# One group in seven fetches its source rows by matmul instead of by gather

## What is computed

```python
def _L0_gnn_ref(h, weight, w_comp, self_loop_weight, A1_w, A1_b, A2_w, A2_b, rel_emb, src, dst, etype):
    x = h[src]                       # one source row of 32 features per edge
    y = h[dst]
    msg = jnp.einsum('eb,ebo->eo', w_comp[etype], jnp.einsum('ei,bio->ebo', x, weight))
    x_hat = x @ A1_w.T + A1_b
    y_hat = y @ A2_w.T + A2_b + rel_emb[etype]
    a = jnp.tanh(jax.nn.relu(jnp.sum(x_hat * y_hat, axis=-1) / scale))
    nei = jax.ops.segment_sum(a[:, None] * msg, dst, num_segments=N)
    last_e = jax.ops.segment_max(jnp.arange(E, dtype=jnp.int32), dst, num_segments=N)
    curr = h[src[last_e]] @ self_loop_weight
    return jax.nn.relu(jnp.where((in_deg > 0)[:, None], nei + curr, jnp.zeros_like(nei)))
```

## Time and profile before

| | |
|---|---|
| three runs | 1352.35, 1353.69 (median), 1355.46 us |
| the profiled execution, its own time | 1355.84 us |
| its span, first to last instruction | 1354.0 us |
| mean granted TensorE clock in it | 0.635 |
| busy: PE, DVE, ACT, POOL | 943.7, 926.2, 636.1, 756.1 us |
| sweep, first fetch to the flag's last step | 75.5 to 1013.7 us |
| instructions | 53620 |

### The profile page before, as it was taken

How to read it: one execution, slowest core, us unless ns; L and a number is a source line. 1 busy time by engine, 2 the same in 40 slices (tenths; PEclk the granted TensorE clock), 3 DMA queues, 4 the chain that set the end, 5 groups by cost and what they waited for, 6 DMA issues and landing times.

```text
span 1354.0 us, 53620 instructions
## 1 busy us (share of the span) xinstructions
PE 943.7 (70%) x21540; PEld 843.1 (62%) x21540; DVE 926.2 (68%) x3188; ACT 636.1 (47%) x1731; POOL 756.1 (56%) x793
## 2 busy tenths in 40 slices
PE   3268777666666666666666666666664696999997
PEld 3257666555555555555555555555554696899997
DVE  8279988666776667667666666666754798555556
ACT  1147766545555555455455545455559783000000
POOL 5777777777777777777777777777750000000000
PEclk9556756555555555555555555555556898999999
DMA  4622111111111111111111111111100000000000
GB/s 99 80 56 55 41 41 40 46 45 39 38 36 33 39 40 40 40 39 40 39 40 39 39 39 40 39 40 39 18 12 14 2 4 2 4 4 4 5 4 17
DMA packets 58572, 44.98 MB, mean 33 GB/s; under 512 B 41920, under 2 KB 54560, under 8 KB 58320
## 3 DMA queue, kind: packets, MB, share of 16 engines
q1 hardware_dynamic: 33296, 28.65, 7.6%
q0 software_dynamic: 25024, 12.86, 6.4%
HBM read 38.37 MB, written 3.07 MB: 31 GB/s over the span
## 4 chain that ended last, share of the span: by engine, by line
POOL 41%; issue 21%; PE 16%; DVE 13%; DMA 6%; SPq 2%; ACT 1%; DVEq 0%; POOLq 0%; ACTq 0%
POOL arena L541 41%; PE ps L757 12%; DMA arena<-line_table 2%; DMA arena<-x_pad,arena 2%; DVE arena L1199 2%; DVE arena L1364 1%; DVE arena L1384 1%; PE ps L680 1%; DVE arena L1197 1%; PE ps L728 1%; DMA agg_table<-arena 1%; SPq L442 1%; DMA dst_parts<-arena 1%; DVE arena L1227 1%; PE ps L626 1%
## 5 line engine op out<-in xcount | busy, mean ns | idle before, releaser
L541 POOL DMA_INDIRECT arena<-x_pad,arena x782 | 754.3, 965 | 238.6 <-issue 236.2
L661 PE MATMUL ps<-arena 128*128 128x175 bf16 (+3 forms) x1567 | 199.1, 297 | 199.6 <-DVE arena L1199 199.1
L680 PE MATMUL ps<-arena 128*32 128x44 f32 (+3 forms) x7832 | 239.8, 262 | 96.2 <-DVE arena L1227 96.1
L661 PEld LDWEIGHTS ps<-arena 128*128 128x128 bf16 x1567 | 146.7, 131 | 217.5 <-DVE arena L1199 216.3
L680 PEld LDWEIGHTS ps<-arena 128*32 128x32 f32 x7832 | 182.1, 156 | 142.9 <-DVE arena L1227 122.5
L1199 DVE TENSOR_SCALAR arena<-pair_no,arena 128x275 bf16<-128x275 f16 (+2 forms) x784 | 237.3, 307 | 0.0
L952 ACT ACTIVATE arena<-arena 128x4 f32<-128x4 f32 x196 | 40.3, 206 | 384.7 <-DVE arena L1213 382.1
L1212 DVE TENSOR_TENSOR arena<-ps,arena 128x132 f32<-128x132 f32 x196 | 57.5, 294 | 238.2 <-DMA arena<-x_pad,arena 235.1
L757 PE MATMUL ps<-arena,adj_words 128*128 128x64 f16 (+1 forms) x6250 | 195.3, 193 | 24.2 <-DVEq L1314 20.9
L757 PEld LDWEIGHTS ps<-arena,adj_words 128*128 128x128 fp8e4 x6250 | 193.1, 98 | 26.2 <-DVEq L1314 21.6
L1227 DVE TENSOR_TENSOR arena<-ps,arena 128x768 f32<-128x768 f32 x196 | 187.9, 959 | 6.7
(11 more groups left out here) (196 smaller groups left out, 1095.0 us busy)
## 6 DMA issues: line engine op xcount, KB each, us to landing
arena<-line_table SPq DMA_DIRECT2D x28, 602.0 KB
arena<-x_pad,arena POOLq DMA_INDIRECT x782, 3.3
arena<-line_table SPq DMA_DIRECT2D x28, 140.0 KB
arena<-dst_parts SPq DMA_DIRECT2D x196, 5.7 KB
agg_table<-arena SPq DMA_DIRECT2D x196, 2.5 KB
dst_parts<-arena SPq DMA_DIRECT2D x1, 918.8 KB, 12.5
feat_table<-rows SPq DMA_DIRECT2D x1, 800.0 KB, 14.5
x<-x_pad SPq DMA_DIRECT2D x1, 400.0 KB
```

Of the source, the lines that this page charges most:

```text
L541: pool.indirect_dma_start(to, None, table, bass.IndirectOffsetOnAxis(ap=index, axis=0)).then_inc(done, 16)
L661: mm = nc.tensor.matmul(ps[:, at + d0 * BLOCKS:at + d1 * BLOCKS], row_hot[:, h, k, :], pair_hot[:, h, k, (d0 - first) * BLOCKS:(d1 - first ...
L680: return nc.tensor.matmul(to.rearrange("p (d m) -> p d m", m=MIX_COLS)[:, :, 0:m1 - m0], rows_of_slot, factors[:, :, m0:m1], start=False, ...
```

## The change

One group of each line but the last, 27 in all (`PICKED`, groups 10, 17, ... 192), is no longer gathered. Its 512 source rows are picked by matmul. The host passes the source numbers of these groups (`pick_rows`); VectorE turns each into a code (the node's row in its block of 128, plus 128 times the number of its set of four blocks), SP stores the codes and loads them per line, broadcast to 128 partitions. VectorE compares them with seven constants into the one-hots `pick_hot` (4 in the second group of a line, 3 in the third). TensorE multiplies these with x, split in three bf16 parts: 21 matmuls of 128 columns in each of the last four groups of a line. In the first group of the next line VectorE multiplies the result in PSUM with a mask that keeps the right one of four blocks, and sums into the group's place in `xp`.

In the preparation the first line's load is requested by SP as soon as the projections are done, ahead of the branch; `q_parts` lies in `aggT` and is stored in two parts (5 and 20 blocks), of which the start of the sweep waits for the first and group 31 for the second; the flag no longer waits for them; `feat_table` is stored only in `run_general`, which this input does not take; two small constants stand in SBUF instead of PSUM.

```diff
+PICK_AT, PICKS = LINE + 3, LINES - 1
+PICKED = range(PICK_AT, PICK_AT + PICKS * LINE, LINE)
+PICK_WIDE = 4
+PICK_DEEP = -(-BLOCKS // PICK_WIDE)
+HOTS_AT = ((1, range(0, 4)), (2, range(4, PICK_DEEP)))
...
+            sp.dma_start(pick_line, pick_rows).then_inc(pick_loaded, 16)
+            sp.wait_ge(codes_made, 1)
+            sp.dma_start(pick_table, pick_codes).then_inc(codes_stored, 16)
...
+            sp.wait_ge(lines_stored, 16)
+            sp.wait_ge(projected, BLOCKS // PROJ_PER_BANK)
+            load_lines(0)
             sp.wait_ge(parts_split, 1)
-            sp.dma_start(dst_parts.rearrange("(b p) (j c) -> p b j c", p=P, j=3), q_parts).then_inc(parts_stored, 16)
-            sp.wait_ge(rows_made, 1)
-            sp.dma_start(feat_table.rearrange("(b p) c -> p b c", p=P), rows[:]).then_inc(rows_stored, 16)
+            by_block = dst_parts.rearrange("(b p) (j c) -> p b j c", p=P, j=3)
+            sp.dma_start(by_block[:, 0:FIRST_STORED], q_parts[:, 0:FIRST_STORED]).then_inc(first_parts_stored, 16)
+            sp.dma_start(by_block[:, FIRST_STORED:BLOCKS], q_parts[:, FIRST_STORED:BLOCKS]).then_inc(parts_stored, 16)
...
+                        if c >= 1:
+                            load_lines(c)
+                        if c < PICKS:
+                            if c >= 2:
+                                sp.wait_ge(pick_hots, c - 1)
+                            sp.dma_start(codes[:, c % 2, :], pick_table[c:c + 1, :].to_broadcast([P, WINDOW]))\
+                              .then_inc(code_in[c % 2], 16)
...
                 for g in range(AHEAD, GROUPS):
-                    pool.wait_ge(mixed_used, g - AHEAD + 1)
-                    gather_group(g)
+                    if g not in PICKED:
+                        pool.wait_ge(mixed_used, g - AHEAD + 1)
+                        gather_group(g)
...
+                def pick_tile(c, k):
+                    if k == 0:
+                        pe.wait_ge(pick_hots, c + 1)
+                        pe.wait_ge(pick_read, c)
+                    at = PICK_AT_BANK + k * PICK_WIDE * FEAT
+                    for j in range(PICK_DEEP):
+                        for t in range(3):
+                            mm = nc.tensor.matmul(ps[:, at:at + PICK_WIDE * FEAT], pick_hot[:, j, k * P:(k + 1) * P],
...
+                    mm.then_inc(pick_out, 1)
...
+                    if g // LINE < PICKS and g % LINE >= LINE - SLOTS:
+                        pick_tile(g // LINE, g % LINE - (LINE - SLOTS))
                     sum_mixed(g)
...
+            split(link, x[:], work[:], [x_parts[:, t, 0:BLOCKS, :] for t in range(3)])
...
-            dve.wait_ge(parts_stored, 16)
             dve.sem_inc(flag_ready, 1)
...
+                def make_pick_hots(c, group):
...
+                    for j in blocks:
+                        last = v.tensor_scalar(pick_hot[:, j, :], codes[:, c % 2, :], pick_no[:, j:j + 1], None, ALU.is_equal)
...
+                def read_picked(c):
+                    dve.wait_ge(pick_out, SLOTS * (c + 1))
+                    n = [P, SLOTS * PICK_WIDE, FEAT]
+                    link(v.tensor_tensor(picked.rearrange("p (w f) -> p w f", f=FEAT),
...
+                    link(v.tensor_reduce(xp[:, PICKED[c] % AHEAD, :, 0:FEAT],
```

More of the change, by code:

```diff
@@ L232, in gnn @@
         side = stay.cut(SIDES * 3 * REL_COLS, BF16, n=SIDE).rearrange("p (u j c) -> p u j c", u=SIDES, j=3)
+        codes = stay.cut(2 * WINDOW, F16).rearrange("p (h e) -> p h e", h=2)
+        pick_mask = stay.cut(PICKS * SLOTS * PICK_WIDE, F16).rearrange("p (c k w) -> p c k w", c=PICKS, k=SLOTS)
+        pick = Carver(aggT, NODES_PAD)
+        pick.at = NODES_PAD - 3 * PICK_DEEP * PICK_WIDE * FEAT // 2
+        x_parts = pick.cut(3 * PICK_DEEP * PICK_WIDE * FEAT, BF16).rearrange("p (t b f) -> p t b f", t=3, f=FEAT)
+        pick.at = 0
+        pick_hot = pick.cut(PICK_DEEP * WINDOW, BF16).rearrange("p (j e) -> p j e", j=PICK_DEEP)
+        q_parts = aggT[:, 0:BLOCKS * 3 * REL_COLS // 2 + 1].bitcast(BF16)[:, 0:BLOCKS * 3 * REL_COLS]\
+            .rearrange("p (b j c) -> p b j c", b=BLOCKS, j=3)
+        picked = work[:].rearrange("p b f -> p (b f)")[:, 0:SLOTS * PICK_WIDE * FEAT]
         prep = Carver(arena, ARENA)
@@ L354, in gnn @@
         side_made = sem("side_made")
+        pick_loaded, codes_made, codes_stored = sem("pick_loaded"), sem("codes_made"), sem("codes_stored")
+        code_in = [sem(f"code_in_{h}") for h in range(2)]
+        pick_hots, pick_out, pick_read = sem("pick_hots"), sem("pick_out"), sem("pick_read")
         lines_ready, fetched = sem("lines_ready"), sem("fetched")
@@ L534, in _ @@
             numbers(side_no[:, 0:1], [[1, 1]], 0, 1)
+            numbers(pick_no[:], [[P, PICK_DEEP]], 0, 1)
             pool.memset(ident[:], 0.0).then_inc(constants_made, 1)
@@ L1168, in run_sweep @@
                 link, step = chain.link, chain.step
-                hot_no_ps, next_no_ps = [ps[:, HOT_NO_AT + n * HOTS:HOT_NO_AT + (n + 1) * HOTS] for n in range(2)]
-                link(v.tensor_copy(hot_no_ps, hot_no[:]))
-                link(v.tensor_scalar(next_no_ps, hot_no[:], 1.0, None, ALU.add))
                 link(v.memset(nothing, 0.0))
@@ L1208, in score_edges @@
                     dve.wait_ge(fetched, g + 1)
-                    tiles = min((g + 1) * SLOTS, TILES) - g * SLOTS
-                    earlier = sum(min((n + 1) * SLOTS, TILES) - n * SLOTS for n in range(g % AHEAD, g, AHEAD))
-                    dve.wait_ge(gathered[g % AHEAD], 16 * (earlier + tiles))
+                    if g not in PICKED:
+                        tiles = sum(min((n + 1) * SLOTS, TILES) - n * SLOTS for n in range(g % AHEAD, g + 1, AHEAD)
+                                    if n not in PICKED)
+                        dve.wait_ge(gathered[g % AHEAD], 16 * tiles)
                     link(v.tensor_tensor(product, fetched_of(g)[:, :, 0:SCORED], xp[:, g % AHEAD], ALU.mult))
@@ L1242, in run_sweep @@
                         make_dst_hot(g // LINE + 1)
+                    for group, (at, _) in enumerate(HOTS_AT):
+                        if g % LINE == at and g // LINE < PICKS:
+                            make_pick_hots(g // LINE, group)
+                    if g % LINE == 0 and 1 <= g // LINE <= PICKS:
+                        read_picked(g // LINE - 1)
                     make_mixed(g)
@@ L1721 @@
         "x_pad": x_pad, "edges": edges,
[L1722 removed]
+        "src_cols": columns(grouped[:, 0]), "pick_rows": grouped[:, 0].reshape(GROUPS, WINDOW)[PICK_AT::LINE][:PICKS], "dst_cols": columns(grouped[:, 1]), "next_cols": columns(after), "bases": bases,
         "dst_rows_in": grouped[:, 1].reshape(LINE_ROWS, -1), "rel_rows_in": grouped[:, 2].reshape(LINE_ROWS, -1),
```

75 lines of the change are left out of this document (57 added, 18 removed).

## The result

| | before | changed |
|---|---|---|
| runs, median (lowest to highest), us | 1353.22 (1352.35 to 1355.46) | 1264.1 (1262.08 to 1265.35) |
| ratio with 95% interval | | 0.9338 [0.932, 0.9355] |
| span of the profiled execution, us | 1354.0 | 1263.6 |
| mean granted TensorE clock | 0.635 | 0.778 |
| last gather starts, flag's reduction, us | 1003.00, 1012.07 | 912.08, 921.16 |

The change saves 89 us; 1269 was forecast, and the result lies inside its range. Behind the flag nothing moved: the dense part takes 342 us as before. Every ratio in this document is against runs of the kernel before that were taken beside it; their median moved between 1351.83 and 1355.3 us, so a saving in us is good to a few us only.

A forecast was written before the change was run, and what follows sets the result against it. Gathers bound the kernel at 35.5 us per line, SP's queue next at 30.06. GpSimd 30.4, SP 30.9 and TensorE 31 made 31.3 per line; flags at 928 instead of 1012.07, 84 us less: 1269 us, range 1240 to 1308.

The forecast's parts named there:

- SP's queue: SyncE's DMA order per line: 30.06 us plus 0.33 to issue the codes and 0.5 for landing, 30.9 us.
- The gap of 13.5 us behind the line load: Sign in SP's transfers: about 13.5 us between two stores in each line, no slack before the next load.
- GpSimd's term: Gathers in the sweep: 108 fewer at 1.267 us save 137 us; 24 per line take 30.4 us, last at 866.
- VectorE slows the gathers: Rival for GpSimd's gathers: 0.1 us more on each, 32.8 us per line, time about 1300; chance 0.05.
- TensorE's charge of 4 us per line: Picking matmuls in groups 3 to 6: 4.4 us per group where VectorE wants 3.4, making a line 31 us.
- The clock answered: TensorE's granted clock in the sweep would rise from 0.51 to 0.6 or 0.7 with the picks.
- my 0.131: Price of one 128-column picking matmul on TensorE at 1.2 GHz: 0.131 us, 11.0 us per line at most.
- VectorE: Added work per line: comparisons 1.84 us, product and reduction 1.35, together 3.2; a line of 26.8 us.
- The constants "nothing": Constants moved out of PSUM change two VectorE instructions of 48 and 336 columns by less than 0.1 us: nothing.
- The start: Preparation: first fetch at about 66 to 68 instead of 75.5, 9 us earlier, some 3 of them lost.
- The sum: Whole sweep: line 4 at 151, line 27 at 871, 57.5 us more to flags at 928, 84 us less.

The follow-up runs named there:

- x5_before_fewer: Kernel before without the gathers of the 27 groups, nothing in their place and no picking: 1241.77 us, 0.917 of before.
- x2_hots_apart: Changed kernel with each line's seven comparisons set one by one between other instructions instead of in runs: 1253.27 us, 0.9273 of before.
- x4_before_compare: Kernel before plus 189 comparisons of 512 columns, in runs of four and three, results unread: 1387.09 us, 1.0257 of before.
- x9_both_one_part: x3_both with one part of x instead of three, so 7 picking matmuls per tile instead of 21: 1222.27 us, 0.9018 of before.
- x3_both: Changed kernel with line loads cut by rows and comparisons set apart, the fastest version that leaves nothing out: 1223.11 us, 0.9049 of before.
- x12_const_sbuf: Kernel before with only its two small constants moved from PSUM (f32) to SBUF (bf16): 1358.99 us, 1.0033 of before.
- x7_old_start: Changed kernel with the start of before, constants still in SBUF: 1265.48 us, 0.9346 of before.
- x6_start_only: Changed kernel with its new start but all groups gathered, without codes, comparisons or picks: 1359.59 us, 1.0043 of before.
- x1_split_lines: Changed kernel with each line load cut by rows, 86 as 80 and 6, 20 as 16 and 4: 1256.93 us, 0.9299 of before.

## Why the prediction was right, and where it was not

The number was right (1264 against 1269), in part by luck: the prediction gave the end to SP's queue and TensorE, and the gathers set it. By its steps:

- **SP's queue: right.** Forecast 30.9 us per line; the loads from line 4 to 26 stand (824.79 - 149.05) / 22 = 30.7 us apart, and x5_before_fewer has 30.03 with neither codes nor picks. The gap of 13.5 us behind the line load is there, with no slack before the next.
- **GpSimd's term: mis-sized.** The step "108 x 1.267 = 137 us. A line now holds 24 gathers: 30.4 us" took the gather's duration as untouched. It became 1.338 us, so 32.1 us per line, and the last gather started at 912, not 866. That is the rival "VectorE slows the gathers", given 0.05: it assumed 0.1 us on each gather, and the run showed 0.07. Its sentence that in the sweep "the rows show no such growth with VectorE busy 98%" was the error. It was true of the instructions there, which are shorter, read PSUM or, like L1182, stand alone in the sweep, and said nothing of a run of four 512-column comparisons. The prediction named the rule by which these "would count as well" and then left it out of the sum. x2_hots_apart and x4_before_compare show it from both sides. The rival's time of 1300 did not come, because it laid its slower line behind line 4; the gathers start at 11 us and need 902 whatever the lines do, and 11 + 902 + 9 is 922, where the flag stood at 921.
- **TensorE's charge of 4 us per line: wrong.** The clock answered as said (0.51 to 0.72), but two thirds of the picks' matmuls are worth 1 to 4 us over the whole sweep (x9_both_one_part), where the term had 4 us in each line. A line of x3_both ahead of the gathers' bound is 27.8 us, against 26.8 from VectorE's terms without that charge (27.3 with the prices measured below). The chain of waits shows both levels for the 21 matmuls of a tile:

```profile
264.07 2.25 PE ps L762 x21
...
268.23 1.18 PE ps L762 x21
```

  The granted clock was 0.50 from 264 to 266.4 us and 1.00 from 268.2 to 269.5. So at 1.2 GHz it is 0.107 us each, at 2.4 GHz 0.056; my 0.131 from the earlier trace rows was a quarter too high. The Trainium skill, "TensorE: Matmul & The Clock Gate", section "Wait — 56ns, not 53.3ns?", states 107 and 56 ns for 128 columns; the trace agrees.
- **VectorE: nearly right.** Forecast 3.2 us per line; measured 1.13 and 0.87 for the two runs of comparisons, 0.68 for the product and 1.03 for the reduction, 3.7 together. The reduction was forecast at 0.64 from a row whose 588 ns is a mean over two shapes (the one of 462 elements took 0.64 alone) and which read PSUM, while this one reads SBUF.
- **The constants "nothing": wrong**, 4 us in the kernel before (x12_const_sbuf).
- **The start: right in size, worthless in effect.** First fetch at 62.3 (forecast 66 to 68), 13 us earlier than before, line 4 at 149.05 (forecast 151). Line 4 is thus later than before's 146.87, and x7_old_start gives the whole start about 1 us.
- **The sum.** The flag stands at 921 where 928 was forecast. The load of line 27 went out at 857 and not at 871: line 4 was 2 us early, and a line took 30.8 us on average and not 31.3, since TensorE did not take its 4 us and the queue alone was left. But from there to the flag it took 64 us and not 57.5: VectorE stood still there for 5.4 us in all until gathers landed, which a sum at its own pace leaves out. In the gathers' terms the result is 137 us for 108 gathers less, minus 46 us for the 69 ns more that each of the other 674 took: 91 us, and the last one starts 91 us earlier. Of the 46, x2_hots_apart gives 41 back. The two errors had opposite signs: a line that was charged too much for TensorE, and gathers that were charged too little, so that their last one came at 912 and not at 866. The best version shows what the reading missed: 41 us lay in the order of VectorE's instructions and the number of rows of one transfer.

## What to carry to other kernels

When an engine that never pauses is the bound, ask first what the change makes slower on it, not only what it removes: count the instructions of other engines that will run beside it, and try a run of them in the kernel before, as x4_before_compare does. When two limits lie within a few per cent of each other, test the edits together; the end follows the later of the two, so alone each edit looks small (7 and 11 us, together 41). How far the last step stands behind each limit's last work tells which one it is (9 us behind the last gather, or 32). And work that starts earlier brings nothing unless it is on the path that sets the end.

## What the runs showed of the hardware

- **A run of wide 16-bit comparisons on VectorE holds GpSimd's indirect DMA up.** One gather takes 0.95 us alone, 1.74 us on average beside a run of four or three of 128x512 from SBUF to SBUF, and 1.16 us where they are 256 columns wide. Set one by one among others, the same comparisons leave the mean of all gathers at 973 ns, against 968 with none (x6_start_only); the 155 gathers that overlap one of them take 0.98. The Trainium skill, "SBUF — State Buffer", section "Who interferes with whom", says that such an operation can, in its two-port modes, take a port pair that VectorE shares with GpSimd, for its whole length, and that the other then waits. The trace agrees for runs, as far as times can show it (no row shows the port); that one alone costs next to nothing is only seen here.
- **Two inputs in SBUF instead of one cost less, but something.** A gather beside the 336-column comparison took 1.12 us in x6_start_only and 1.07 in x12_const_sbuf, against 0.97 with the constant in PSUM, where it was f32 and not bf16.
- **86 rows go over two DMA engines.** In the packet records of the changed kernel's line 4, from 152 to 162 us, two packets of 7168 bytes are under way at any time, with a median of 272 ns: 43 rows on each of two engines would take 11.7 us (an estimate), the last one ends at 164.4, and two of the store's packets end only at 164.8. Cut into 80 and 6 rows, sixteen are under way at once, all 106 rows of the two loads land within 4.3 us, and the gap between the first two stores falls from 13.5 to 3.7 us (x1_split_lines). The Trainium skill, "DMA: Bandwidth & Descriptors", section "Why a DMA increments its semaphore by 16 and not by 1", has the rule: the engines used are the largest number up to 16 that divides the rows. For 86 that is 2 and for 80 it is 16; the trace agrees. The prediction had taken the gap of 13.5 us as given.
